# One decoder layer on one Trainium2 core: the recurrent part of each step moved to other places of the step, and its POOL work cut in two

## What is computed

```python
x_prev = shift(x)                                  # along the 16 positions
k, v, r = ((mu * x + (1 - mu) * x_prev) @ W.T for each of three mu, W)
# recurrence over the 16 positions, per feature, of exp(k) and exp(k) * v
wkv = sigmoid(r) * numerator / denominator @ W_out.T
x = layernorm(x + wkv)
x = layernorm(x + cross_attention(x, ctx_768))     # 16 heads of width 16, 256 queries x 256 keys a position
x = layernorm(x + moe(x))                          # grouped top-4 of 16 experts, and a shared expert of twice the width
```

## Time and profile before

| | |
|---|---|
| median of 3 executions | 1193.81 us (1188.74 to 1201.66) |
| profiled execution | 1184.75 us, of which span 1182.9 us |
| PE busy | 1069.7 us (90%) |
| DVE busy | 834.8 us (71%) |
| ACT, POOL busy | 659.3 us (56%), 611.8 us (52%) |
| mean granted TensorE clock | 0.949 |

### The profile page before, as it was taken

One profiled execution on the slowest core, in us unless ns is written; L12 is line 12 of the kernel. 1 busy time (PEld: TensorE's weight loads), 2 busy tenths in 40 slices (PEclk: granted clock), 3 DMA queues, 4 the chain that ended last, 5 costly groups with the idle time before them and its releaser, 6 DMA issues.

```text
span 1182.9 us, 21592 instructions
## 1 busy us (share of the span) xinstructions
PE 1069.7 (90%) x6580; PEld 818.2 (69%) x6580; DVE 834.8 (71%) x1688; ACT 659.3 (56%) x2000; POOL 611.8 (52%) x660
## 2 busy tenths in 40 slices
PE   4788999999999999999997999999999999888883
PEld 2455767677676776766665788778777788777762
DVE  2275698997979989889795756757565452666686
ACT  0157566666666675666565576676677544434310
POOL 5435337475474754846545557375534355546600
PEclk8579899999999999999898999999999999999997
DMA  9504053341532413112212213222322354778363
GB/s 257 183 12 148 1 166 103 102 159 55 167 114 90 158 54 109 54 38 72 78 51 85 70 64 96 91 94 78 96 80 88 110 155 128 250 226 265 109 213 107
DMA packets 95710, 135.38 MB, mean 114 GB/s; under 512 B 10962, under 2 KB 79473, under 8 KB 95600
## 3 DMA queue, kind: packets, MB, share of 16 engines
q1 hardware_dynamic: 82544, 101.53, 28.2%
q0 software_dynamic: 13056, 32.47, 7.5%
HBM read 61.91 MB, written 76.23 MB: 117 GB/s over the span
## 4 chain that ended last, share of the span: by engine, by line
PE 64%; DVE 20%; ACT 5%; issue 4%; DMA 3%; SPq 2%; POOL 1%; DVEq 0%; POOLq 0%; ACTq 0%
PE bS L742 9%; PE bT L569 8%; PE bM L555 7%; PE bY L799 6%; PE bO L763 4%; DVE Sc L1263 3%; DVE nmx L1265 3%; PE bU L672 3%; DVE acc L1475 3%; PE bM L603 3%; PE bU L562 3%; PE bM L562 3%; PE bC L842 2%; PE bU L699 2%; PE bT L799 2%
## 5 line engine op out<-in xcount | busy, mean ns | idle before, releaser
L1263 DVE TENSOR_SCALAR Sc<-bS 128x1024 f32<-128x1024 f32 x128 | 155.2, 1213 | 143.8 <-PE bS L742 143.3
L1018 ACT ACTIVATE Sc<-Sc,nmx 128x256 f32<-128x256 f32 x512 | 252.8, 500 | 0.0
L1026 ACT ACTIVATE PT<-bT 128x512 f32<-128x512 f32 x256 | 151.4, 592 | 166.0 <-PE bT L569 162.1
L569 PE MATMUL bT<-idn,Sc 128*128 128x128 f32 x1024 | 168.6, 289 | 10.2 <-ACT PT L1026 9.6
L1575 POOL TENSOR_TENSOR rstd<-vpe,mhalf 128x2 f32<-128x2 f32 x48 | 34.4, 717 | 276.9 <-DVE vpe L1186 276.6
L569 PEld LDWEIGHTS bT<-idn,Sc 128*128 128x128 f32 x1024 | 115.5, 144 | 85.7 <-issue 54.6
L1265 DVE TENSOR_REDUCE nmx<-Sc 128x4 f32<-128x1024 f32 x128 | 156.2, 1220 | 4.4
L742 PE MATMUL bS<-KT,QT 32*128 32x256 f32 x1024 | 151.2, 414 | 1.8 <-DVE Sc L1263 1.8
L1632 POOL DMA_INDIRECT Xs<-x,slots x120 | 118.6, 988 | 35.7 <-issue 18.4
L555 PE MATMUL bM<-mix,Wp 128*128 128x256 f32 x384 | 103.1, 416 | 18.5 <-POOL mix L1594 8.1
L742 PEld LDWEIGHTS bS<-KT,QT 32*128 32x128 f32 x1024 | 90.6, 191 | 40.3 <-issue 30.7
(11 more groups left out here) (213 smaller groups left out, 2080.4 us busy)
## 6 DMA issues: line engine op xcount, KB each, us to landing
Xs<-yg SPq DMA_DIRECT2D x16, 1768.0 KB, 9.2
xb<-Xs SPq DMA_DIRECT2D x152, 136.0 KB, 2.2
yg<-Yt SPq DMA_DIRECT2D x30, 512.0 KB, 4.4
W<-w SPq DMA_DIRECT2D x4, 1152.0 KB, 11.6
xTs<-xT SPq DMA_DIRECT2D x16, 256.0 KB, 2.9
x<-x SPq DMA_DIRECT2D x16, 256.0 KB, 4.1
Base<-stg SPq DMA_DIRECT2D x15, 256.0 KB, 2.1
acc<-Base SPq DMA_DIRECT2D x15, 256.0 KB, 3.5
```

What stands on the lines that cost most here:

```text
L569: last = pe.transpose(dst[:, j, t * P:(t + 1) * P], src[:, t, j * P:(j + 1) * P], idn[:, :])
L1018: last = fn(Sc[:, n % 3, m, t, :], Sc[:, n % 3, m, t, :], ACT.Exp, bias=nmx[:, n % 3, m, t:t + 1], accum_out=rs[:, s % 2, t, h:h + 1])
L1026: fn(flat(PT[:, h % RING]), bT[:, :], ACT.Copy).then_inc(a_pt.sem, 1)
L1263: ts(Sc[:, n % 3].rearrange("p m t k -> p (m t k)"), flat(bS[:, :, :]), CLAMP, -CLAMP, ALU.min, ALU.max).then_inc(d_clip.sem, 1)
```

## The change

- POOL: `mixes` becomes `mix_kv` (difference, mix of k, mix of v; five operations), now the first of the step, and `mix_r` (two operations), behind the third group of sends. `sums` moves up behind `pairs(3)`, and waits in addition for `project_out(a)`, for the norm of position a (`d_x1`) and for that of position t (`d_x2`). `add_bo` moves down. Nothing is added or removed.
- PE: K moves from slot 5 to the end of slot 0, V from slot 6 to the end of slot 1, R from slot 7 to slot 6; `context_v` moves ahead of the second transpose of slot 1. Waits change accordingly.
- DVE: both `invert`s of position b in slot 4 of step s, instead of slots 0 and 1 of the next step; `weigh_k` in slot 2 instead of 6.
- ACT: `exp_k` in slot 0, `tanh_r` in slot 6, `copy_v` ahead of the second probability copy.
- SP: `load_turned` in slot 7 instead of 4; `fill` in 64 quarters, one a slot, instead of 16 wholes, two a step.

```diff
 # SP
-                if 0 <= s < E // 2 and g in (1, 6):
-                    fill(2 * s + g // 6)
+                if 0 <= s < E // 2:
+                    fill(8 * s + g)
                 if 0 <= a < L and 0 <= b < L and g == 4:
-                    if s + 3 < L:
-                        load_turned(s + 3)
                     load_context(b)
+                if 0 <= a < L and s + 3 < L and g == 7:
+                    load_turned(s + 3)
...
 # PE, first_part
-                        pe.wait_ge(a_q.sem, a_q.at(s - 1))
+                        pe.wait_ge(a_thr.sem, a_thr.at(s - 1))
+                    if s >= 4:
+                        pe.wait_ge(d_slots.sem, d_slots.at(s - 4))
...
+                    if s >= 2:
+                        pe.wait_ge(a_v.sem, a_v.at(s - 2))
                     proj(M, Wp[:, WV], mix[:, 1], ND).then_inc(p_kvr.sem, 1)
...
                     pe.wait_ge(g_mix.sem, g_mix.at(s, 3))
-                    pe.wait_ge(d_ekv.sem, d_ekv.at(s))
+                    if s:
+                        pe.wait_ge(a_q.sem, a_q.at(s - 1))
+                    else:
+                        pe.wait_ge(d_ekv.sem, d_ekv.at(s))
                     proj(M, Wp[:, WR], mix[:, 2], ND).then_inc(p_kvr.sem, 1)
...
 # PE, project_out
+                if s + 1 < L:
+                    pe.wait_ge(d_ekv.sem, d_ekv.at(s + 1))
...
 # DVE, slot
-                if A and g == 0:
-                    invert(a, 0)
+                if B and g == 4:
+                    invert(b)
+                if B and g == 2:
+                    weigh_k(b)
-                if B and g == 6:
-                    weigh_k(b)
...
 # POOL
+            def mix_kv(s):
+                if s >= 4:
+                    pool.wait_ge(d_slots.sem, d_slots.at(s - 4))
                 pool.wait_ge(s_xT[s % 2], 16 * (s // 2 + 1))
                 if s:
                     pool.wait_ge(p_kvr.sem, p_kvr.at(s - 1))
...
             def sums(s):
                 pool.wait_ge(a_ek.sem, a_ek.at(s))
                 pool.wait_ge(d_ekv.sem, d_ekv.at(s))
+                if s:
+                    pool.wait_ge(p_wout.sem, p_wout.at(s - 1))
+                    pool.wait_ge(d_x1.sem, d_x1.at(s - 1))
+                if s >= 3:
+                    pool.wait_ge(d_x2.sem, d_x2.at(s - 3))
...
                 pairs(0)
+                if B:
+                    mix_kv(b)
+                pairs(1)
                 send(s - 2, 0)
-                pairs(1)
                 pairs(2)
                 if T:
                     rsqrt(1, t)
-                send(s - 2, 1)
                 if A:
                     rsqrt(0, a)
+                send(s - 2, 1)
                 pairs(3)
-                if A:
-                    add_bo(a)
+                if B:
+                    sums(b)
                 pairs(4)
                 send(s - 2, 2)
                 if B:
-                    mixes(b)
+                    mix_r(b)
                 pairs(5)
+                if A:
+                    add_bo(a)
                 send(s - 2, 3)
                 pairs(6)
-                if B:
-                    sums(b)
                 pairs(7)
```

More of the change, by code:

```diff
@@ L95 @@
 SPARE = DENSE * TOK * TOPK
+FILLS = [EPOCHS[1].cap // P * q // 4 for q in range(5)]
 LAST_T = {TAIL: 0, TAIL + 1: 1, TAIL + 2: 2, TAIL + 4: 3, TAIL + 5: 4, TAIL + 9: 5, TAIL + 10: 6, TAIL + 11: 8}
@@ L449, in fill @@
                 e = EPOCHS[1]
-                sp.dma_start(Xs[e.k][n * e.cap:(n + 1) * e.cap].rearrange("(r p) d -> p r d", p=P),
-                             blank.rearrange("p (a d) -> p a d", a=1).to_broadcast([P, e.cap // P, ROW])).then_inc(s_fill, 16)
+                sp.wait_ge(p_s.sem, p_s.at(n))
+                first, rows = n // 4 * e.cap + FILLS[n % 4] * P, (FILLS[n % 4 + 1] - FILLS[n % 4]) * P
+                sp.dma_start(Xs[e.k][first:first + rows].rearrange("(r p) d -> p r d", p=P),
+                             blank.rearrange("p (a d) -> p a d", a=1).to_broadcast([P, rows // P, ROW])).then_inc(s_fill, 16)
             def pad(e):
@@ L466, in fetch @@
                     if e.k:
[L467 removed]
+                        sp.wait_ge(s_fill, 16 * 4 * E)
                 if i >= XBUFS:
@@ L868, in slot @@
                     t_chunk(t, 1)
+                if 0 <= s < L and g == 1:
+                    context_v(s)
                 if T and g == 2:
@@ L877, in slot @@
                 if B and g == 6:
-                    first_part(b, 1)
-                if B and g == 7:
                     first_part(b, 2)
@@ L898, in slot @@
                     turn_probs(n, 1)
-                if 0 <= s < L and g == 1:
-                    context_v(s)
+                if B and g == 0:
+                    first_part(b, 0)
+                if B and g == 1:
+                    first_part(b, 1)
                 if A and g == 2:
@@ L910, in slot @@
                     t_chunk(t, 5)
-                if B and g == 5:
-                    first_part(b, 0)
                 if T and g == 6:
@@ L1109, in slot @@
                     copy_q(a)
-                if B and g == 7:
+                if B and g == 6:
                     tanh_r(b)
@@ L1121, in slot @@
                     exps(n + 1, 1)
+                if 0 <= s < L and g == 1:
+                    copy_v(s)
                 if heads:
@@ L1126, in slot @@
                     t_chunk(t, 0)
-                if 0 <= s < L and g == 1:
-                    copy_v(s)
+                if B and g == 0:
+                    exp_k(b)
                 if T and g == 3:
@@ L1134, in slot @@
                     t_chunk(t, 5)
-                if B and g == 5:
-                    exp_k(b)
                 if T and g == 6:
@@ L1235, in weigh_k, with invert @@
                 tt(ekv, ek, M, ALU.mult).then_inc(d_ekv.sem, 1)
-            def invert(s, j):
-                if j == 0:
-                    dve.wait_ge(g_den.sem, g_den.at(s))
-                dve.reciprocal(den[:, j, :], den[:, j, :]).then_inc(d_rden.sem, 1)
+            def invert(s):
+                dve.wait_ge(g_den.sem, g_den.at(s))
+                for j in range(ND):
+                    dve.reciprocal(den[:, j, :], den[:, j, :]).then_inc(d_rden.sem, 1)
             def finish_wkv(s):
@@ L1578, in final_rsqrt, with mix_one, mix_r @@
                 rsqrt(2 + l % 4, l // 4)
-            def mixes(s):
+            def mix_one(s, m):
+                mu = vec[:, m, :].rearrange("p (j a) -> p j a", a=1).to_broadcast([P, ND, TOK])
+                pool.tensor_tensor(mix[:, m], dx, mu, ALU.mult).then_inc(g_dmix.sem, 1)
+                pool.wait_ge(g_dmix.sem, g_dmix.at(s, m + 1))
+                pool.tensor_tensor(mix[:, m], mix[:, m], xTs[:, 1 - s % 2], ALU.add).then_inc(g_mix.sem, 1)
+            def mix_kv(s):
+                if s >= 4:
+                    pool.wait_ge(d_slots.sem, d_slots.at(s - 4))
                 pool.wait_ge(s_xT[s % 2], 16 * (s // 2 + 1))
-                now, before = xTs[:, s % 2], xTs[:, 1 - s % 2]
                 if s:
                     pool.wait_ge(p_kvr.sem, p_kvr.at(s - 1))
-                pool.tensor_tensor(dx, now, before, ALU.subtract).then_inc(g_dx.sem, 1)
+                pool.tensor_tensor(dx, xTs[:, s % 2], xTs[:, 1 - s % 2], ALU.subtract).then_inc(g_dx.sem, 1)
                 pool.wait_ge(g_dx.sem, g_dx.at(s))
-                for m in range(3):
-                    mu = vec[:, m, :].rearrange("p (j a) -> p j a", a=1).to_broadcast([P, ND, TOK])
-                    if m == 2:
-                        pool.wait_ge(g_dmix.sem, g_dmix.at(s, 2))
-                    pool.tensor_tensor(mix[:, m], dx, mu, ALU.mult).then_inc(g_dmix.sem, 1)
-                    pool.wait_ge(g_dmix.sem, g_dmix.at(s, m + 1))
-                    pool.tensor_tensor(mix[:, m], mix[:, m], before, ALU.add).then_inc(g_mix.sem, 1)
+                for m in range(2):
+                    mix_one(s, m)
+            def mix_r(s):
+                pool.wait_ge(g_dmix.sem, g_dmix.at(s, 2))
+                mix_one(s, 2)
             def sums(s):
```

20 lines of the change are left out of this document (10 added, 10 removed).

## The result

The changed kernel is slower: 1268.4 us median against 1191.28, ratio 1.069 with a 95% interval of 1.063 to 1.075. (1191.28 is the kernel before once more, now the median of four executions.) Ratios that have an interval are taken over each kernel's executions in the chip's faster state alone, so they can differ a little from the quotient of the medians. The direction was forecast, the size was not: 1230 us in a range that ended at 1258. The profiled execution of the changed kernel took 1262.08 us, span 1260.3, mean granted clock 0.94 (before 1184.75, 1182.9, 0.95). The working of the prediction came to 1226 for an execution like the profiled one, so 36 us of the 38 can be looked for in this trace.

A forecast was written before the change was run, and what follows sets the result against it. Dense steps were taken as bound by a loop of nearly full DVE and PE, routed steps by PE. Opening +10, steps 2 to 9 +38, step 10 -1, step 11 -6 gave 1226, plus 4: 1230 us, range 1200 to 1258.

The forecast's parts named there:

- the price of the half clock: Steps 2 to 9: PE's gap before R lowers the granted clock in most steps; 1.7 us a step, bounds 0 and 3.4.
- the 0 for steps 12 to 14: Routed steps 12 and 13: PE has other work before R; 0, bounds 0 and +3; step 14 untouched.
- POOL's chain: Norms' end to R's mix: 14.5 us against PE's 11.5, PE stands 3.0 before R; 1212 to 1245, chance 0.60.
- The loop of 51.4: Clean step around the new loop: 25.4 + 14.5 + 5.1 + 6.4 = 51.4 us, against 47.7.
- half of slot 7 is waiting anyway: Slot 7: argument against the clock falling twice a step, a case given chance 0.15.
- Step 11: Step 11: first routed rows come early; -6.8 and about -3.4, against +3.7 of the loop: -6 us.
- The opening: Up to step 2: R of position 0 comes behind sums, first project_out 50.8; +10 us, bounds 0 and +17.
- DVE: DVE: reciprocals move to idle slot 4, router operations lose 6.7 us of waiting on POOL; DVE stops being the bound.
- The third case: Dense steps: POOL's chain does not hold PE, norms and sums 3 us sooner; step 48.4, up to 1195; chance 0.14.
- the clock falling twice a step: Dense steps: this, or first mix and load_turned late; 1.7 to 2 us more a step, 1245 to 1265; chance 0.15.

The follow-up runs named there:

- e1: Changed kernel with mix_r put right behind mix_kv in POOL's step, ahead of the sums; 1204.88 us, ratio 1.025.
- e6: Changed kernel with useless PE matmuls in slot 6 of steps 2 to 9, two ahead of the transpose, three ahead of R; 1237.26 us, ratio 1.055.
- e5: Kernel of e4 with ACT's copy_v ahead of slot 1's exponentials instead of behind them; 1201.21 us, ratio 1.026.
- after_again: Changed kernel run once more, unaltered, for its trace, on a chip where the kernel before takes 1172.72; 1246.38 us, ratio 1.063.
- e2: Changed kernel with one and a half extra projections on PE ahead of its wait for R's mix in steps 2 to 9; 1247.73 us, ratio 1.059.
- e11: Changed kernel with half of K left out in steps 3, 4, V in 5, 6, R in 8, 9; steps 3 to 6 54.4 to 54.6 us.
- e4: Kernel of e1 with PE's projection R moved from slot 6 to slot 5, K's old place; 1202.18 us, ratio 1.026.
- e10: Kernel before with SP's part alone, leaving out V (steps 4, 5), R (6, 7), K (8, 9); without R 49.7 and 51.6 us a step instead of 47.7.
- e8: Kernel of e5 with DVE's two reciprocals back in slots 0 and 1 of the next step; 1229.02 us, ratio 1.031.
- after: First profiled execution of the changed kernel, nothing further altered; 1262.08 us.
- e9: Kernel before with SP's part alone, plus the turn of x2 and ACT's copy of it moved to slot 4; four executions of 1205.81 to 1242.83 us.

## Why the prediction came out as it did

The step that failed is the price of the half clock: 1.7 us a step in the sum, 3.3 measured. The second is the 0 for steps 12 to 14, where V's wait costs 5.6. The mechanism, POOL's chain holding R back, was right.

- **POOL's chain: right.** From the end of the norms (581.90 + 1.37 = 583.27) to the end of R's mix (597.90) 14.6 us, forecast 14.5. R waited for it in seven of the eight steps, and with the mix made early (e1) the step lost 3.6.
- **The loop of 51.4: right in each piece.** Slot 0 to the norms 25.2 (forecast 25.4), POOL 14.6 (14.5), R to the end of slot 6 6.9 (5.1 + half clock), slot 7 7.9 (6.4 + half clock). PE's idle time before R was 1.32 + 1.59 = 2.9, forecast 3.0. But the forecast put all of it down to POOL, and 1.32 is a wait for ACT, which stood there without POOL's too (e1).
- **The clock: the term that was mis-sized.** Taken: 1.7 a step, with bounds 0 and 3.4. Measured: R at 3.13 and L713 at 3.45 with matmuls around them, 54.65 - 51.4 = 3.3 a step, the upper bound. This is +13 us over eight steps. The sentence "half of slot 7 is waiting anyway", which spoke against a second fall, was wrong: the clock fell there in seven of eight steps. e6 shows the link between the wait and the half clock for R. For slot 7 no run shows it: with the same two short waits (0.78 and 0.35) L713 is at full clock in all eight steps of e1, and at half clock in five of e6, where slot 6 has no wait above 0.33. The Trainium skill's rule that was cited (TensorE: Matmul & The Clock Gate, "HAM oscillation — how this bites in real kernels") led the right way here: the price recurred in every step. It doesn't tell which waits have it.
- **Steps 12 and 13 at "0, bounds 0 and +3": wrong.** +5.6 over steps 12 to 14 is V behind `copy_v`, as e5 shows. The prediction counted that wait (0.2) in dense steps only and said of the routed ones that PE has other work. It has, but that stands behind V in PE's queue: 1.98 us of waiting in a step in which PE is otherwise busy 70.9 of 71.3. The other 14 us, in waits with no named releaser, could not have been worked out from the trace before, which has none of that kind in these steps.
- **Step 11: right. The opening: right in kind, its size in part by luck.** Step 11 gave -8.0 for -6. The opening cost +10.4 for +10 in this pair of traces, and the first project_out started at 48.5 for 50.8. But in the four other traces with POOL's order as changed (`after_again`, e2, e6, e11) step 2 starts at 178.7 to 179.8 instead of 174.4. That is within the bounds given, nearer to the upper one.
- **DVE: right in kind, and worth nothing.** 3.1 us a step less busy. L1353's successor takes 0.17 instead of 0.87. Operations that meet POOL still wait: `L1322`, with two SBUF inputs on 32 columns, takes 1.20 and ends at 597.96, just after the second operation of R's mix (597.90), where its like beside it (`L1320`) takes 0.18. So the Trainium skill's rule on the port (SBUF — State Buffer, "Who interferes with whom") agrees with the trace. What was freed was not on the loop.
- **The third case's price: wrong.** It put a loop without POOL's wait at 48.4. e1 and e4 put it at 50.7 at the least. Subtracting a wait from a loop is valid only down to the next holder, and there were two more behind it (ACT's queries and exponentials, DVE's hidden row). The prediction saw that K and V cost 3.7 to 3.9 in slots 0 and 1, but not that they had cost next to nothing where they were; only leaving them out showed that (e10).
- **The range.** The case that came true, the clock falling twice a step, was in the list with 1245 to 1265 and a chance of 0.15. The range was cut inside it, at 1258. The median of 1268.4 lies above even that case, which has nothing for the routed steps: not V's 5.6 us, and not the waits with no named releaser.

How the +51.7 of steps 2 to 9 divides: 22.5 is the changed placement at nearly full clock (e4: 409.1), which the runs explain by K and V moving out of waits into full slots. The other 29 is POOL's order with the half clock that its wait brings: e1 took it all away (409.5). e6 got 12 of it back by keeping PE busy during the same waits.

## What to carry to other kernels

Work that stands in a wait can be free, and may be holding the clock up; before moving it, leave it out where it is and see what the step does. In this kernel no step became shorter when one of three projections of 1.7 us was left out of its old slot, and two of them made it longer. In their new slots two of them, K and V, cost their full length. When a loop is added up around a new wait, list every wait that it hides, and give the half clock bounds for each wait in the loop rather than a price once a step.

## What the runs showed of the hardware that was not expected

- Less work made the step longer: without R 49.7 and 51.6 us instead of 47.7, PE's matmuls at half clock behind a wait of 1.56 us. And with 0.9 to 1.7 us of work taken out of the changed kernel the step stayed at 54.4 to 54.6, since the half clock reached over more of it.
- Which waits bring the clock down is not told by their length. A wait of 1.34 us before the turn of x2 stands in every step of the kernel before: in six of eight the matmuls behind it run at full clock, in steps 4 and 5 a stretch of half clock begins within 2 us. Alone before R, 1.32 us was followed by half clock in five of eight steps (e1); 1.94 us in the same slot of e4 in none. The waits of 0.78 and 0.35 in slot 7 were followed by half clock in no step of e1, in two of e4 and in all eight of e8.
- In one set of traces ACT and DVE stood for up to 7.5 us in routed steps with no releaser that the trace names (`after`, e8, e9, e10). Any comparison of routed steps between two traces should look for these first.
